# An attention block with routed experts on one core: other order and shorter forms in the routing between attention and the expert layer

## What is computed

```python
x = L0_attn_x                                  # (4, 512, 256)
h = _layernorm(x) * (1 + ca) + sa
x = x + ga * attention(h)                      # 16 heads
h = _layernorm(x) * (1 + cb) + sb
x = x + gb * ffn(h)

def ffn(x):                                    # 2048 tokens, 16 experts
    scores = sigmoid(xt @ gate_w.T)
    # the best 2 of 4 groups (by the maximum in a group), and in them the best 4 experts
    w = w / w.sum()                            # of the chosen four
    g = silu(h1) * h3 * combine                # per expert, inner width 176
    return g @ W2 + shared_ffn(x)
```

## Time and profile before

| | us |
|---|---|
| runs | 1024.6, 1026.63, 1023.91 |
| median | 1024.6 |
| the profiled execution | 1026.2 |
| its span | 1024.4 |

### The profile page before, as it was taken

The page is one execution under the profiler, slowest core; times in us unless marked ns, Lnnn a source line. Parts: engine busy times, 40 slices in busy tenths (PEclk is TensorE's granted clock), DMA queues, the critical chain, the costliest instruction groups (busy, mean ns, idle before and its releaser), DMA issues.

```text
span 1024.4 us, 19916 instructions
## 1 busy us (share of the span) xinstructions
PE 876.5 (86%) x6996; PEld 744.5 (73%) x6996; DVE 733.5 (72%) x1596; ACT 573.9 (56%) x1071; POOL 675.8 (66%) x641
## 2 busy tenths in 40 slices
PE   5678889999999999999999988449974999999920
PEld 5546568888878888788887877438853899999910
DVE  5766997878887788786879775664843566666656
ACT  1335667788787877887787876422310444444400
POOL 3664667888888788887887975505675355555544
PEclk9889989999999999999999998858996899999965
DMA  7561421333523235232325253323222333333264
GB/s 289 195 155 34 148 44 40 81 79 80 155 44 85 55 85 174 48 81 48 85 54 155 48 205 113 100 51 114 88 106 107 109 115 122 116 120 119 82 236 174
DMA packets 65757, 111.20 MB, mean 109 GB/s; under 512 B 16918, under 2 KB 43293, under 8 KB 63821
## 3 DMA queue, kind: packets, MB, share of 16 engines
q1 hardware_dynamic: 46905, 69.24, 25.3%
q10 hardware_dynamic: 11843, 22.84, 6.3%
q0 software_dynamic: 6912, 17.84, 4.5%
HBM read 46.06 MB, written 39.58 MB: 84 GB/s over the span
## 4 chain that ended last, share of the span: by engine, by line
PE 60%; DVE 12%; DMA 9%; POOL 9%; issue 6%; ACT 3%; SPq 0%; POOLq 0%; DVEq 0%; ACTq 0%
PE bank L677 13%; PE bank L679 11%; PE bank L678 11%; PE bank L857 7%; DMA slots<-h,slot_i 7%; PE bank L1072 7%; PE bank L834 4%; POOL p_lo L1896 3%; POOL slots L1951 2%; PE bank L1044 2%; PE bank L931 2%; DVE nmax L1243 2%; POOL turns L1874 1%; DVE turns L1216 1%; POOL h_hl L1852 1%
## 5 line engine op out<-in xcount | busy, mean ns | idle before, releaser
L1896 POOL TENSOR_TENSOR p_lo<-p_f,p_hi 128x512 f16<-128x512 f32 x256 | 326.4, 1286 | 57.3 <-ACT p_f L1634 56.8
L1243 DVE TENSOR_REDUCE nmax<-bank 128x1 fp32r<-128x512 f32 x256 | 174.6, 686 | 96.2 <-PE bank L834 92.6
L1631 ACT ACTIVATE p_hi<-bank,log_up 128x512 f16<-128x512 f32 x256 | 176.2, 688 | 114.4 <-PE bank L679 105.5
L1634 ACT ACTIVATE p_f<-bank,log_up 128x512 f32<-128x512 f32 x256 | 175.3, 685 | 11.3 <-POOL p_lo L1896 11.3
L857 PEld LDWEIGHTS bank<-vals,p_hi 128*128 128x128 f16 x2048 | 111.1, 98 | 54.2 <-issue 27.0
L857 PE MATMUL bank<-vals,p_hi 128*128 128x66 f16 x2048 | 139.6, 195 | 10.1 <-POOL p_lo L1896 9.6
L1874 POOL TENSOR_TENSOR turns<-turns 128x512 f32<-128x512 f32 x64 | 90.8, 1420 | 66.9 <-DVE turns L1217 66.9
L1223 DVE TENSOR_TENSOR qk<-rows_f,qk 128x512 fp32r<-128x512 f32 (+1 forms) x128 | 131.9, 1030 | 2.2
L677 PE MATMUL bank<-qk 128*128 128x512 f32 x256 | 123.4, 482 | 11.1 <-issue 10.2
L857 PE MATMUL bank<-vals,p_lo 128*128 128x66 f16 x1024 | 121.8, 194 | 0.0
L834 PE MATMUL bank<-qk 128*128 128x512 f32 x256 | 104.6, 410 | 3.7 <-DVE nmax L1243 3.6
(11 more groups left out here) (229 smaller groups left out, 2133.2 us busy)
## 6 DMA issues: line engine op xcount, KB each, us to landing
rows_f<-turns SPq DMA_DIRECT2D x64, 256.0 KB, 3.9
slots<-pad ACTq DMA_DIRECT2D x4, 2880.0 KB, 10.1
h<-slots SPq DMA_DIRECT2D x80, 144.0 KB
w_hi<-parts SPq DMA_DIRECT2D x16, 512.0 KB, 8.5
rows_f<-kl_f SPq DMA_DIRECT2D x32, 192.0 KB, 3.0
w_raw<-in_w ACTq DMA_DIRECT2D x4, 1408.0 KB, 11.8
h_dram<-h_hl SPq DMA_DIRECT2D x3, 1024.0 KB, 3.9
qk<-lat_st SPq DMA_DIRECT2D x16, 192.0 KB, 4.0
```

Source lines behind the costliest of these rows:

```text
L1243: dve.tensor_reduce(nmax[:, k % MAXES:k % MAXES + 1], max_bank[q % 2][:], AX_X, ALU.max, negate=True)\
L1631: act.activation(p_hi[:, u % TB, :], score_bank[u % 2][:], ACT.Exp, bias=log_up[:, 0:1], scale=SCALE)
L1634: act.activation(p_f[:, u % 2, :], score_bank[u % 2][:], ACT.Exp, bias=log_up[:, 0:1], scale=SCALE)\
L1896: pool.tensor_tensor(p_lo[:, u % TB, :], p_f[:, u % 2, :], p_hi[:, u % TB, :], ALU.subtract).then_inc(s_pl, 1)
```

## The change

The statistics of the last batch are put ahead of most of the routing of the other batches. `best_experts` loses its first two operations to a new `count_rivals`, which for `first` stands between the statistics of rows 0, 1 and rows 2, 3. The last sum of `choose` is written twice: first to a float16 table `chosen_h`, which signals `masked`, then to `above`. ScalarE makes a float16 copy `sums_h` of a triangle and ones; the triangle's table is now minus one on and below the diagonal and zero above it, so that its product with `chosen_h`, added to the running sum through the tile, gives the same place as before. `count()` takes both float16 tables. `places()` drops a copy, a subtraction and a scaling. The picks, reduction and cast are done for the first 4 tiles and then for the other 12, with one signal each; GpSimd starts its first 16 scatters on the first signal and waits for the second before the 17th. All others wait for both signals.

```diff
-            sp.wait_ge(indexed, 1)
+            sp.wait_ge(indexed, 2)
             sp.dma_start(w2_s[:, 8:13], w2[:, 8:13]).then_inc(ld_w2, 16)
...
             def count():
-                chosen = above.rearrange("p t e -> p e t")
-                pe.matmul(bank[6][:, 0:NT * E], tri_s, chosen, start=True, stop=True)
-                pe.matmul(bank[6][:, NT * E:], ones_s, chosen, start=True, stop=True).then_inc(counted, 1)
+                chosen = chosen_h.rearrange("p t e -> p e t")
+                pe.wait_ge(halved, 1)
+                pe.matmul(bank[6][:, NT * E:], sums_h[:, P:], chosen, start=True, stop=True)
+                pe.matmul(bank[6][:, 0:NT * E], sums_h[:, 0:P], chosen, start=True, stop=True).then_inc(counted, 1)
...
-            pe.wait_ge(masked, 1)
+            pe.wait_ge(masked, 2)
             count()
...
-            pe.wait_ge(indexed, 1)
+            pe.wait_ge(indexed, 2)
...
-                ins = dve.tensor_tensor(above[:, t], sums, above[:, t], ALU.add)
-                if t.stop == NT:
-                    ins.then_inc(masked, 1)
-                    dve.wait_ge(masked, 1)
-                else:
-                    chain(ins)
+                dve.tensor_tensor(chosen_h[:, t], sums, above[:, t], ALU.add).then_inc(masked, 1)
+                chain(dve.tensor_tensor(above[:, t], sums, above[:, t], ALU.add))
...
+                first_tile = tiles_of[:, 0]
+                dve.memset(first_tile[:, 0:1], 0.0)
                 chain(dve.tensor_tensor_scan(sums, keep_s, bank[6][:, NT * E:], 0.0, ALU.mult, ALU.add))
-                chain(dve.tensor_copy(loads, by_expert[:, :, NT - 1]))
-                chain(dve.tensor_tensor(by_expert, by_expert, in_tile, ALU.subtract))
-
-                chain(dve.tensor_tensor(place, loads.unsqueeze(2).to_broadcast([P, E, NT]),
+                chain(dve.tensor_tensor(place, by_expert[:, :, NT - 1:NT].to_broadcast([P, E, NT]),
                                         full_s.unsqueeze(1).to_broadcast([P, E, NT]), ALU.is_gt))
...
-                chain(dve.tensor_scalar(scaled, first_tile, float(P), None, ALU.mult))
-                chain(dve.tensor_tensor(place, by_expert, within_tile, ALU.add))
-                chain(dve.tensor_tensor(place, place, scaled[:, 0:E].unsqueeze(2).to_broadcast([P, E, NT]), ALU.add))
+                chain(dve.tensor_tensor(place, by_expert, behind, ALU.add))
+                chain(dve.scalar_tensor_tensor(out=place, in0=first_tile[:, 0:E].unsqueeze(2).to_broadcast([P, E, NT]), scalar=float(P),
+                                               in1=place, op0=ALU.mult, op1=ALU.add))
                 other = place.rearrange("p e t -> p t e")
-                for r in range(TOPK):
-                    ins = dve.scalar_tensor_tensor(out=picked[:, :, r, :], in0=msk, scalar=float(r), in1=other,
-                                                   op0=ALU.is_equal, op1=ALU.mult)
-                chain(ins)
-                chain(dve.tensor_reduce(slot_f, picked, AX_X, ALU.add))
-                dve.tensor_copy(slot_i[:], slot_f).then_inc(indexed, 1)
+                for part in (slice(0, TB), slice(TB, NT)):
+                    for r in range(TOPK):
+                        ins = dve.scalar_tensor_tensor(out=picked[:, part, r, :], in0=msk[:, part], scalar=float(r), in1=other[:, part],
+                                                       op0=ALU.is_equal, op1=ALU.mult)
+                    chain(ins)
+                    chain(dve.tensor_reduce(slot_f[:, part], picked[:, part], AX_X, ALU.add))
+                    dve.tensor_copy(slot_i[:, part], slot_f[:, part]).then_inc(indexed, 1)
...
+            second_statistics(LAST, 0)
+            second_statistics(LAST, 1)
+            count_rivals(first)
+            second_statistics(LAST, 2)
+            second_statistics(LAST, 3)
             best_experts(first)
-            for q in range(TB):
-                second_statistics(LAST, q)
             choose(first)
...
             act.wait_ge(s_pl, UNITS)
+            act.wait_ge(ld_t, 32)
+            act.activation(sums_h, tri_ones, ACT.Copy).then_inc(halved, 1)
...
             pool.wait_ge(indexed, 1)
             for t in range(NT):
+                if t == TB:
+                    pool.wait_ge(indexed, 2)
...
-    tab[:, R_TRI:R_ONES] = np.triu(np.ones((P, P), np.float32), 1)
+    tab[:, R_TRI:R_ONES] = np.triu(np.ones((P, P), np.float32), 1) - 1.0
```

More of the change, by code:

```diff
@@ L204, in program @@
         early_s = table[:, R_EARLY:R_TRI]
-        tri_s = table[:, R_TRI:R_ONES]
+        tri_ones = table[:, R_TRI:R_TOKEN]
         ones_s = table[:, R_ONES:R_TOKEN]
@@ L311, in program @@
         den = quota
+        halves_at = (6 * E + TOPK + 1) * NT
+        chosen_h = held[:, halves_at:halves_at + NT * E // 2].bitcast(F16).rearrange("p (t e) -> p t e", t=NT)
+        sums_h = held[:, halves_at + NT * E // 2:halves_at + NT * E // 2 + P].bitcast(F16)
         own_i = sb("own_i", [P, SLOT_TILES], I32)
@@ L386, in program @@
             ("padded", "pad_set", "masked", "listed", "indexed", "extended"))
+        halved = sem("halved")
         sent = [sem(f"sent{j}") for j in range(IN_FLIGHT)]
@@ L1344, in best_groups, with count_rivals @@
                 chain(dve.tensor_tensor(equal[:, t].rearrange("p t (a b) -> p t a b", a=EG), rival, me, ALU.is_equal))
-            def best_experts(t):
+            def count_rivals(t):
                 n = t.stop - t.start
@@ L1349, in best_experts @@
                 chain(dve.tensor_tensor(above[:, t], above[:, t], equal[:, t], ALU.add))
+            def best_experts(t):
+                n = t.stop - t.start
                 chain(dve.tensor_reduce(gsel[:, t], above[:, t].rearrange("p t (a b) -> p t a b", a=EG), AX_X, ALU.add))
@@ L1402, in places @@
                 dve.wait_ge(ld_f, 16)
-                within_tile = bank[6][:, 0:NT * E].rearrange("p (e t) -> p e t", e=E)
-                in_tile = bank[6][:, NT * E:].rearrange("p (e t) -> p e t", e=E)
+                behind = bank[6][:, 0:NT * E].rearrange("p (e t) -> p e t", e=E)
                 sums = pre_a.rearrange("p t e -> p (t e)")
@@ L1413, in places @@
                                         full_s.unsqueeze(1).to_broadcast([P, E, NT]), ALU.is_gt))
                 chain(dve.tensor_reduce(tiles_of[:, 1, 0:E], place, AX_X, ALU.add))
-                dve.memset(tiles_of[:, 0, 0:1], 0.0)
-                chain(dve.tensor_tensor_scan(tiles_of[:, 0, 1:], ones_s[:, 0:E], tiles_of[:, 1, 0:E], 0.0, ALU.mult, ALU.add))
-                first_tile, scaled = tiles_of[:, 0], tiles_of[:, 1]
-                chain(dve.tensor_scalar(scaled, first_tile, float(P), None, ALU.mult))
@@ L1426, in places @@
-                chain(dve.tensor_reduce(slot_f, picked, AX_X, ALU.add))
-                dve.tensor_copy(slot_i[:], slot_f).then_inc(indexed, 1)
+                chain(dve.tensor_tensor_scan(first_tile[:, 1:], ones_s[:, 0:E], tiles_of[:, 1, 0:E], 0.0, ALU.mult, ALU.add))
+                chain(dve.tensor_tensor(place, by_expert, behind, ALU.add))
+                chain(dve.scalar_tensor_tensor(out=place, in0=first_tile[:, 0:E].unsqueeze(2).to_broadcast([P, E, NT]), scalar=float(P),
+                                               in1=place, op0=ALU.mult, op1=ALU.add))
@@ L1509, in _ @@
             best_groups(last)
+            count_rivals(last)
             best_experts(last)
@@ L1790, in shared_position @@
                     if t == 0:
-                        act.wait_ge(indexed, 1)
+                        act.wait_ge(indexed, 2)
                     high_weights(e)
```

## The result

The changed kernel takes 1019.7 us, the median of 20 runs (1015.8 to 1024.7). The kernel before took 1026.4 beside it (20 runs, 1022.9 to 1035.8). The ratio is 0.9938, with an interval from 0.992 to 0.9957: 6.4 us less, between 4.4 and 8.2. Forecast was 1019.2 of 1024.6, a ratio of 0.9947.

What follows compares the result with a forecast made beforehand. The bound was taken as the chain from attention's end to the first scatter, then 64 scatters to the first load of slots. Terms 2.3 + 0.15 + 2.95 gave 5.4 us less: median 1019.2 of 1024.6, range 1017.3 to 1022.4.

Steps and rivals of the forecast that it cites:

- Statistics first: VectorE after attention: last batch's statistics ahead of other routing make the last variance 2.3 us earlier, L1348's successor held by GpSimd.
- the old gap of 0.46: VectorE's wait of 0.46 us between the last statistics and the aggregates (L1304), taken over unchanged from the old profile.
- Counts, 0.15: Two count products on TensorE in float16: 0.30 us of VectorE idle removed, 0.15 paid for a second sum; gain 0.15.
- half precision nearly worthless here: At the counts: float16 matters little, as VectorE sat idle for only 0.30 us there; gain never more than 0.30.
- Places, 2.96: Chain in `places()`, 7.24 us: removed steps save 0.87, the scaling sum returns 0.16, four-tile picks save 2.25; gain 2.96.
- The sum with scaling: In `places()`: the sum that takes the scaling in was to take 583 ns against 0.42 us, giving 0.16 back.
- Its toll moves but stays: First scatters: the load of second weights meets the third instead of the first; the fifth starts 5.3 to 5.6 us earlier.
- the first rival: First scatters: the load of second weights catches the second scatter and the fourth waits; gain 3.9, time 1020.7; chance 0.12.
- has a head start: First scatters: argument that the second scatter, issued near 686.3 against the load's 686.65, would not be stuck.
- VectorE's picks hold GpSimd back: First scatters: picks with two SBUF inputs beside GpSimd for 2.8 us; scatters only 2.6 earlier, time 1022.0; chance 0.08.
- Slack of 8.2: Shared expert's end to the slots' first load: 11.0 us of slack before, 8.2 left, so its shift of 2.6 is hidden.
- the forecast of 5.4: Gain ahead of the first scatter, 2.3 + 0.15 + 2.95, taken to reach the kernel's end in full: 5.4 us less.

Runs made afterwards that it cites:

- e3: Changed kernel with picks, reduction and cast in one part for all 16 tiles, both signals at its end; ratio 0.9939 to the kernel before.
- e5: Changed kernel with the load of second weights issued behind the running sum over tiles, not the second signal; ratio 0.9906 to the kernel before, median 1016.5 us.
- e8: Kernel before with only the load of second weights moved early, behind the running sum over tiles; ratio 0.9936 to the kernel before.
- e2: Changed kernel with the last batch's statistics put back behind the maxima of `first`; ratio 0.9947 to the kernel before.
- e9: Changed kernel with three of five late experts' weights in the first loads, only two behind the running sum over tiles; ratio 0.9918 to the kernel before.
- e6: Changed kernel with the load of second weights early, behind the running sum, and picks, reduction and cast in one part; ratio 0.9906 to the kernel before.

## Why the prediction was right, and where not

- **The time** came as forecast, 0.9938 against 0.9947, inside the interval. Of its steps, those ahead of the first scatter hold and the one behind it failed.
- **Statistics first, 2.3.** Right in its mechanism: L1353, not the statistics, is held by GpSimd's addition, and ends at the forecast 0.21 behind it. Measured 2.73, by undoing 2.83. The mis-sized term is "the old gap of 0.46": it shrank to 0.10. Of the way from there to the logits another 0.18 went, which was not followed. Logits idle for 2.79, forecast 2.7.
- **Counts, 0.15.** Measured 0.23 in the stretch and 0.35 by undoing: TensorE saves 1.0, and VectorE's own ranks hide the rest. The forecast "half precision nearly worthless here" stands.
- **Places, 2.96.** Measured 7.24 - 4.22 = 3.02. The sum with scaling took 0.42, not 583 ns, and the four picks 0.79, not 0.63; the two errors cancel. The second signal came 2.78 behind the first, forecast 2.8.
- **"Its toll moves but stays … the fifth starts 5.3 to 5.6 earlier".** This step failed. It took the load to meet the third scatter, with two already landed. The load is issued 1.88 behind the first scatter's start (684.30 against 682.42) and the second scatter, which starts 0.16 later, is caught: the first rival, given 0.12. The fourth starts at 38.74, and the fifth gains 3.79. That rival had a gain of 3.9. The reason given against it, that the second scatter "has a head start", was false, in part because the first took 1.75. e3, e5 and e8 show that it is the load: the split is lost against it, and taking it away gives 4.3 to 4.9 there by itself. By the Trainium skill (DMA: Bandwidth & Descriptors, Queues, rings and completion order) a DMA engine takes turns between queues packet by packet and drains a whole packet before it switches. By that a load would slow a scatter and not block it; the 9.33 of the second scatter agrees but does not prove it, since no run here shows the order of the packets.
- **VectorE's picks hold GpSimd back.** Real but small: 1.22 becomes 1.74 in most traces, 1.34 and 1.35 in two (e2, e9). The Trainium skill (SBUF — State Buffer, SBUF: two separate sides) says that a VectorE instruction with two SBUF inputs and a GpSimd one that reads SBUF exclude each other for the whole of the one that started first; L1353 agrees, ending behind the addition, and the first scatter agrees in direction, though 1.66 of picks cost it 0.1 to 0.5.
- **Slack of 8.2.** Read from one trace as a bound, and it is none. In the traces of most experiments the shared expert ended last. Its start moves by 3.38, forecast 2.6. The sum also left out that the load of slots waits for the shared expert's twelfth tile (`listed`), which held it in four traces.
- **The size of the whole gain is not settled.** By the marks the change gives 3.4 where the shared expert bounds and about 3.8 at the fifth scatter; the profiled execution after won 2.40 by the load of slots, and 1.58 ahead of the stretch. Measured are 6.4 [4.4, 8.2], and 0.9933 and 0.9926 in the repeats. One trace more or less moves the later marks by as much: the last scatter starts 2.4, 5.2 and 3.2 earlier than before in the three traces of the changed kernel, and the scatters take 99.4 to 102.3 from first to last in them, 98.5 before. That the forecast of 5.4 met the time is thus partly luck: 5.4 was the sum at the head, and it does not reach the end by the way described.

The best by its ratio is e5 (with e6), 0.9906 [0.9872, 0.994] against the change's 0.9938 [0.992, 0.9957]: the load earlier by a wait on its true last reader. Its fifth scatter is surely earlier; that the kernel is faster than the changed one is likely and not shown, as the intervals overlap.

## What to carry to other kernels

When small transfers are started earlier, look what large load is let go by the same signal or near it: it can take all that was won, and moving that load to the last true reader of its memory may be worth as much as the edit. Work that runs beside the bound has slack only in the trace that was read; see how long it lasts in several executions before it is called covered, and read in the code every semaphore that the next stage's first instruction waits for. Compare stages from a common event and not from the start of the span: the marks then repeat to hundredths where whole times differ by several us.

## What the runs showed of the hardware

- A load of 880 KB over 88 partitions on SyncE's queue makes one scatter in flight land after 7.6 to 9.3 instead of about 2.3, and GpSimd wait 5.3 to 6.8 for it, at the start or in the middle. Issued 3.3 ahead of the scatters it costs 2.36, 5.6 ahead nothing (0.50, the usual wait). With it early, the 64 scatters took 90.1 to 94.9 from first to last, otherwise 97.0 to 102.3.
- Idle time ahead of the aggregates depends on what stands before: 0.46 behind four statistics in a row, 0.10 behind two and two with products between. Why is open.
- Two 128x256 products took 1.08 from float16 tables and 2.06 from float32 ones, at a granted clock of 0.50.
- The shared expert, the same 412 instructions on TensorE each time, took from 85 to 118 in different executions. TensorE's granted clock in it was 0.90 to 0.93 where it took 85 to 93, and 0.80 to 0.87 where it took 98 to 118; cause and effect are not separated.
